# Banded attention in a fused two-layer kernel: three one-pass products of split operands for the projections, their differences on GpSimd, and the turned tiles moved one step ahead

## The reference, cut to what matters

```python
x = x + _L1_attn_b_ref(_layernorm(x), Wqkv, bqkv, Wout, bout)

qkv = (x @ Wqkv.T + bqkv).reshape(B, S, 3, H, d).transpose(2, 0, 3, 1, 4)
q, k, v = (qkv[0], qkv[1], qkv[2])
kp = jnp.pad(k, ((0, 0), (0, 0), (pads, pads), (0, 0)))      # pads = 64
...
scores = jnp.einsum('bhncd,bhnld->bhncl', qc, kb) / np.sqrt(d)
band = (j >= c) & (j < c + WIN)                               # WIN = 128
attn = jax.nn.softmax(jnp.where(band, scores, -jnp.inf), axis=-1)
o = jnp.einsum('bhncl,bhnld->bhncd', attn, vb).reshape(B, H, S, d)
o = o.transpose(0, 2, 1, 3).reshape(B, S, D)
return o @ Wout.T + bout
```

## Time and profile before

| | |
|---|---|
| time, median of 3 runs | 3794.84 us (3794.36 to 3796.17) |
| time of the profiled execution | 3795.73 us |
| its span, first to last instruction | 3793.8 us |
| mean granted TensorE clock | 0.968 of full |
| busy over the span: PE, PEld, DVE, ACT, POOL | 92%, 81%, 62%, 56%, 39% |
| first and last instruction of the changed stage's products | 2896.4 us, 3614.5 us |

### The profile page before, as it was taken

How to read it: one execution, slowest core, us unless ns; L and a number is a source line. 1 busy time by engine, 2 the same in 40 slices (tenths; PEclk the granted TensorE clock), 3 DMA queues, 4 the chain that set the end, 5 groups by cost and what they waited for, 6 DMA issues and landing times. The chain is left out here.

```text
span 3793.8 us, 115662 instructions
## 1 busy us (share of the span) xinstructions
PE 3506.4 (92%) x44514; PEld 3086.2 (81%) x44514; DVE 2371.0 (62%) x6503; ACT 2117.6 (56%) x6528; POOL 1471.5 (39%) x2245
## 2 busy tenths in 40 slices
PE   8948999799839999799999999999998999999998
PEld 7838999677629999798899999999976777777777
DVE  6774555688765554455444444444456888888894
ACT  3345555545446555344444444444444888888895
POOL 3444665210035655344454444444444222222215
PEclk9978999899969999999999999999998999999999
DMA  3143443411153443300000000000000000000002
GB/s 122 42 139 98 93 93 68 135 52 46 63 186 80 93 93 79 88 3 3 3 3 3 3 3 3 3 3 3 3 6 16 2 2 2 2 2 2 2 2 94
DMA packets 137900, 164.61 MB, mean 43 GB/s; under 512 B 11392, under 2 KB 127264, under 8 KB 137376
## 3 DMA queue, kind: packets, MB, share of 16 engines
q1 hardware_dynamic: 112800, 123.81, 10.1%
q0 software_dynamic: 24576, 33.57, 5.3%
HBM read 97.18 MB, written 60.16 MB: 41 GB/s over the span
## 5 line engine op out<-in xcount | busy, mean ns | idle before, releaser
L2290 ACT ACTIVATE wa_S<-wa_S,wa_top 128x256 f32<-128x256 f32 x1024 | 511.8, 507 | 138.8 <-DVE wa_top L2354 137.9
L1912 DVE TENSOR_TENSOR so_raw<-so_rows,so_masks 128x1024 f32<-128x1024 f32 x256 | 313.6, 1225 | 227.9 <-PE so_rows L1612 219.6
L2354 DVE CUSTOM_DVE_ANT_0 wa_S<-wa_bank,wa_band 128x256 f32<-128x256 f32 x1024 | 366.9, 420 | 8.4 <-issue 8.3
L1991 POOL TENSOR_TENSOR so_more<-so_compact,so_head 128x384 f32<-128x384 f32 x224 | 185.5, 828 | 338.3 <-PE so_bankC L1694 307.5
L2213 PE MATMUL wa_bank<-ident,wa_S 128*128 128x128 f32 x2048 | 275.3, 276 | 21.0 <-ACT wa_probT L2297 21.0
L2213 PEld LDWEIGHTS wa_bank<-ident,wa_S 128*128 128x128 f32 x2048 | 231.9, 141 | 65.8 <-ACT wa_S L2290 29.7
L1901 DVE SCALAR_TENSOR_TENSOR so_compact<-so_compact,so_bankX 128x96 f32<-128x96 f32 x192 | 48.9, 255 | 355.5 <-PE so_bankX L1730 355.5
L1828 ACT COPY so_O<-so_bankC 128x128 f32<-128x128 f32 x256 | 68.4, 267 | 307.8 <-PE so_bankC L1694 307.8
L1996 POOL TENSOR_TENSOR so_OT<-so_O,so_OT 128x128 fp32r<-128x128 f32 x256 | 117.5, 459 | 307.3 <-ACT so_OT L1834 307.3
L626 POOL DMA_INDIRECT sum_dram<-y,rows x128 | 223.5, 1746 | 29.4 <-issue 27.2
L704 ACT ACTIVATE m4e_hT<-m_bank,m4e_bias 128x256 fp32r<-128x256 f32 x256 | 126.4, 494 | 153.2 <-PE m_bank L656 146.0
(11 more groups left out here) (452 smaller groups left out, 10171.7 us busy)
## 6 DMA issues: line engine op xcount, KB each, us to landing
m_w_raw<-in_L_ffn_W_dram SPq DMA_DIRECT2D x64, 512.0 KB
sum_dram<-X SPq DMA_DIRECT2D x16, 1024.0 KB, 4.5
X<-sum_dram SPq DMA_DIRECT2D x16, 1024.0 KB, 7.8
X<-in_L_attn_a_x_dram SPq DMA_DIRECT2D x8, 1024.0 KB, 11.3
xn_dram<-m2r_xn SPq DMA_DIRECT2D x16, 512.0 KB, 4.5
sp_gx<-gate_dram SPq DMA_DIRECT2D x64, 128.0 KB, 2.7
xn_dram<-m4r_xn SPq DMA_DIRECT2D x16, 512.0 KB, 4.7
out_dram<-X SPq DMA_DIRECT2D x8, 1024.0 KB, 4.4
```

The source lines that it names most:

```text
L1912: nc.vector.tensor_tensor(AB[:, t % 2].rearrange("p h m t -> p h (m t)"), rows4[:, :, 0:2 * P], masks[:].rearrange("p m t -> p (m t)")[:, ...
L1991: nc.gpsimd.tensor_tensor(state[:, t % UT], compact[:, t % UT, :, None, :].broadcast_to([P, 3, HG, DK]), head[:, None, :, None].broadcast_ ...
L2290: nc.scalar.activation(S[:, n % 2, z], S[:, n % 2, z], ACT.Exp, bias=top[:, n % 2, z:z + 1], scale=-1.0, accum_out=sums[:, i % 2, SET * c ...
L2354: nc.vector.tensor_tensor_reduce(out=S[:, n % 2, z], in0=bS[g][:, eo * SPAN:(eo + 1) * SPAN], in1=band[:], scale=-(D ** -0.5), scalar=3e38 ...
```

## The change

1. The weights `wT` and the turned tiles `xnT` become pairs of fp32r tensors, high part and low part, and each product is the sum of high by high, high by low and low by high: six matmuls of 128x512 per query or key item in place of two fp32 ones, and twelve of 128x256 per value item in place of four.
2. ScalarE makes the high part of a turned item by its copy, and then a second, plain copy of the same bank into `xT_raw`, a single buffer. GpSimd subtracts (`low_xT`), and products wait for `xT_low`.
3. The weights are loaded into `wT_raw`, which lies in the memory of `S`; in the prologue ScalarE makes their high parts in two pieces, and VectorE the low ones.
4. The turned items are now 0, 1, 2 and 6, and the query and key products 3, 4, 5 and 7 to 11.
5. The tile that wraps around is taken whole from an edge that GpSimd copies behind the sequence, so item 15 has no halves.
6. `share_all`, `RT`, `y` and `xT_raw` lie in resident buffers; `share_all` has one buffer in place of two, so that `spread_share(i)` waits for `turn_share(i-1)` (`RT_done`).

```diff
-    ACT_ITEMS, DVE_ITEMS = (0, 1, 6, 7), (2, 3, 4, 5, 8, 9, 10, 11, 12, 13, 14, 15)
+    TURNS, PRODUCTS = (0, 1, 2, 6), (3, 4, 5, 7, 8, 9, 10, 11)
+    ACT_ITEMS, DVE_ITEMS = TURNS, PRODUCTS + (12, 13, 14, 15)
+    PARTS = ((0, 0), (0, 1), (1, 0))
+    XRING = 4
...
-        wT = sb("wT", [P, HC, 3 * HID])
+        wT = sb("wT", [P, 2, HC, 3 * HID], F32R)
+        W_PIECES = (slice(0, 2 * HID), slice(2 * HID, 3 * HID))
...
-        xn, xnT = sb("xn", [P, 4, HID]), sb("xnT", [P, HC, PADDED])
+        xn, xnT = sb("xn", [P, XRING, HID]), sb("xnT", [P, 2, HC, SEQ + EDGE], F32R)
...
+        wT_raw = S[:].rearrange("p a z k -> p (a z k)")[:, 0:HC * 3 * HID].rearrange("p (c r) -> p c r", c=HC)
+        y, xT_raw = R.y[:, 0], R.y[:, 1]
+        share_all, RT = (R.L[:].rearrange("p i e -> p (i e)")[:, n * HID:(n + 1) * HID] for n in range(2))
...
+                def low_xT(p):
+                    m = on_act(p)
+                    pool.wait_ge(s_["act_item"], m + 1)
+                    nc.gpsimd.tensor_tensor(turned_part(1, p), xT_raw, turned_part(0, p).bitcast(F32), ALU.subtract
+                                            ).then_inc(s_["xT_low"], 1)
+                    if p % ITEMS == TURNS[-1]:
+                        pool.wait_ge(s_["xT_low"], m + 1)
+                        nc.gpsimd.tensor_copy(xnT[:, :, :, 0:EDGE], xnT[:, :, :, SEQ:SEQ + EDGE]).then_inc(s_["xT_edge"], 1)
...
-                    if i >= 2:
-                        pool.wait_ge(s_["RT_done"], i - 1)
+                    if i >= 1:
+                        pool.wait_ge(s_["RT_done"], i)
...
-                for i in range(TB + 4):
+                for i in range(4):
                     normalize(i)
+                for m, p in enumerate(TURNS):
+                    if m >= 1 and 2 * m + 3 < TB:
+                        normalize(2 * m + 2)
+                        normalize(2 * m + 3)
+                    low_xT(p)
                 spread_Q(0)
+                for i in range(TB, TB + 4):
+                    normalize(i)
                 for i in range(NT + 2):
+                    b, j = divmod(i, TB)
+                    more = b + 1 < BATCH
+                    after = TB * (b + 1)
+                    if j == 1 and more:
+                        low_xT(ITEMS * (b + 1) + 1)
                     if i + 1 < NT:
                         spread_Q(i + 1)
                     if 2 <= i < NT + 2:
                         residual(i - 2)
                     if 1 <= i <= NT:
                         spread_share(i - 1)
-                    if i + TB + 4 < NT:
-                        normalize(i + TB + 4)
+                    if j in (0, 1, 2, 4) and more:
+                        new = after + {0: 4, 1: 6, 2: TB, 4: TB + 2}[j]
+                        if new < NT:
+                            normalize(new)
+                            normalize(new + 1)
+                    if 2 * j in TURNS and more:
+                        low_xT(ITEMS * (b + 1) + 2 * j)
...
-                    elif k < 12:
-                        half, e = k // 6, (k - 2) % 6
-                        pe.wait_ge(s_["act_item"], on_act(ITEMS * b + (2 if half == 0 else 8)))
+                    elif k in PRODUCTS:
+                        half, e = divmod(PRODUCTS.index(k), 4)
+                        pe.wait_ge(s_["xT_low"], len(TURNS) * b + (2 if half == 0 else 4))
                         at = EDGE + half * HALF
-                        for c in range(HC):
-                            last = nc.tensor.matmul(to[:], wT[:, c, e * P:(e + 1) * P], xnT[:, c, at:at + HALF],
-                                                    start=(c == 0), stop=(c == HC - 1))
+                        steps = [(u, v, c) for u, v in PARTS for c in range(HC)]
+                        for n, (u, v, c) in enumerate(steps):
+                            last = nc.tensor.matmul(to[:], wT[:, u, c, e * P:(e + 1) * P], xnT[:, v, c, at:at + HALF],
+                                                    start=(n == 0), stop=(n == len(steps) - 1))
...
+                    m = on_act(p)
+                    turned = of[:].rearrange("p (a c t) -> p a c t", a=2, c=HC)
+                    nc.scalar.copy(turned_part(0, p).rearrange("p c (a t) -> p a c t", a=2), turned)
+                    if m >= 1:
+                        act.wait_ge(s_["xT_low"], m)
+                    nc.scalar.copy(xT_raw.rearrange("p c (a t) -> p a c t", a=2), turned).then_inc(s_["act_item"], 1)
+
+                def high_w(n):
+                    nc.scalar.copy(wT[:, 0, :, W_PIECES[n]], wT_raw[:, :, W_PIECES[n]]).then_inc(s_["w_high"], 1)
...
+                for n, piece in enumerate(W_PIECES):
+                    dve.wait_ge(s_["w_high"], n + 1)
+                    nc.vector.tensor_tensor(wT[:, 1, :, piece], wT_raw[:, :, piece], wT[:, 0, :, piece].bitcast(F32), ALU.subtract
+                                            ).then_inc(s_["w_ready"], 1)
```

More of the change, by code:

```diff
@@ L2166, in item @@
                         at = EDGE + half * HALF
-                        for c in range(HC):
-                            last = nc.tensor.matmul(to[:], wT[:, c, e * P:(e + 1) * P], xnT[:, c, at:at + HALF],
-                                                    start=(c == 0), stop=(c == HC - 1))
-                    else:
-                        pe.wait_ge(s_["act_item"], on_act(ITEMS * b + 8))
+                        steps = [(u, v, c) for u, v in PARTS for c in range(HC)]
+                        for n, (u, v, c) in enumerate(steps):
+                            last = nc.tensor.matmul(to[:], wT[:, u, c, e * P:(e + 1) * P], xnT[:, v, c, at:at + HALF],
+                                                    start=(n == 0), stop=(n == len(steps) - 1))
+                    else:
+                        pe.wait_ge(s_["xT_low"], len(TURNS) * (b + 1))
+                        steps = [(u, v, c) for u, v in PARTS for c in range(HC)]
+                        if k == ITEMS - 1:
+                            pe.wait_ge(s_["xT_edge"], b + 1)
@@ L2172, in item @@
                         for a in range(2):
-                            block_at = 2 * (k - 12) + 1 + a
+                            block_at = (2 * (k - 12) + 1 + a) % TB
                             cols = slice(a * HID, (a + 1) * HID)
[L2175 to L2183, removed]
+                            for n, (u, v, c) in enumerate(steps):
+                                last = nc.tensor.matmul(to[:, cols], xnT[:, u, c, block_at * P:(block_at + 1) * P], wT[:, v, c, 2 * HID:],
+                                                        start=(n == 0), stop=(n == len(steps) - 1))
@@ L2236, in turn_share @@
                     for c in range(HC):
-                        last = nc.tensor.transpose(bO[:, HID + c * P:HID + (c + 1) * P], share_all[:, i % 2, c * P:(c + 1) * P], R.ident[:])
+                        last = nc.tensor.transpose(bO[:, HID + c * P:HID + (c + 1) * P], share_all[:, c * P:(c + 1) * P], R.ident[:])
                     last.then_inc(s_["RT_done"], 1)
@@ L2246, in _ @@
                 for p in range(ITEMS):
-                    if p == 2:
-                        pe.wait_ge(s_["qkv_loaded"], 16)
+                    if p in (PRODUCTS[0], 12):
+                        pe.wait_ge(s_["w_ready"], 2 if p == 12 else 1)
                     item(p)
@@ L2280, in item @@
                     act.wait_ge(s_["item_done"], p + 1)
-                    at = EDGE + item_tiles(k)[0] * P
-                    nc.scalar.copy(xnT[:, :, at:at + 2 * P].rearrange("p c (a t) -> p a c t", a=2),
-                                   of[:].rearrange("p (a c t) -> p a c t", a=2, c=HC)).then_inc(s_["act_item"], 1)
+                    m = on_act(p)
[6 more added lines that the diff above has]
+                    nc.scalar.copy(wT[:, 0, :, W_PIECES[n]], wT_raw[:, :, W_PIECES[n]]).then_inc(s_["w_high"], 1)
                 def exponent(n, z):
```

50 lines of the change are left out of this document (27 added, 23 removed).

## The result

The changed kernel takes 3774.72 us (median of five runs, 3772.48 to 3779.7) against 3796.17 (3794.36 to 3800.93) for the kernel before on the same chip: a ratio of 0.9944, with a 95% interval of 0.9934 to 0.9955.

What follows compares the result with a forecast made beforehand. Odd product steps were taken as PE's own, even ones as held by a DVE and ACT chain; -0.69 us a sequence, -4.8 over seven, and +0.5 in the prologue gave -4.3, so 3790.5 us, range 3780 to 3801.

Steps and rivals of the forecast that it cites:

- Step 7: Loop step given the moved product: waits 0.88 us for GpSimd's difference, 5.50 to 7.36 us, +1.86 a sequence.
- odd product steps: Odd loop steps 5, 9, 11 and 13, set by PE's own work: 6.99 less 0.30 each, -1.20 us a sequence.
- fourth rival: Slower: GpSimd's difference is late in step 7; 1.7 us later makes the kernel over 0.2% slower; chance 0.06.
- price of an item: PE's saving per split product item: 0.30 us, between 0.24 and 0.37, so an item of 1.42 us.
- the ring: Loop chain of step end, DVE copies and item, masks, ACT exponentials and copies, PE: 5.58 us whatever PE's item costs.
- Even product steps: Five even loop steps with a product: PE alone 5.41 us, held at 5.58, 0.13 saved each, -0.65 a sequence.
- step 38: Even turn step of the earlier trace: 1.29 us less PE work, still 5.58 us, after a wait for ACT.
- second rival: The ring gives way as DVE's and ACT's work moves up with PE's: near 3781 us; chance 0.14.
- Steps 1, 2, 3 and 6: Loop steps: 1 and 2 ACT-bound at 5.84 (+0.47 together), 3 at 6.48 (-0.51), 6 staying at 5.58 us.
- Step 15: Last step of a loop sequence, loses its item's halves too: 7.35 to 6.69 us, -0.66.
- The prologue: Before the loop: items save 3.6 us against later first product and waits; +0.5 us taken, between -2 and +5.

Runs made afterwards that it cites:

- run 3: Changed kernel, but in the loop step 7's product also waits for the difference of item 6's turn, which it does not need; 3780.72 us.
- run 1: Changed kernel with its products back in fp32, the new order, ScalarE's second copy and GpSimd's differences kept; 3806.63 us, ratio 1.0028 to the kernel before.
- run 5: Changed kernel with two of the three products, a third of each item's matmuls left out; 3750.09 us.
- run 4: Changed kernel with split products but the items in the order of before (turns 0, 1, 6, 7); 3791.5 us.
- run 7: Changed kernel with VectorE's statistics moved from the end of odd steps to behind the fourth mask of even steps; 3773.03 us.
- run 8: As run 7, with VectorE's item also written out behind the second mask of the next step; 3759.9 us, ratio 0.9898 to the kernel before.
- run 9: Kernel before (fp32 products) with VectorE's item behind the next step's second mask and statistics behind even steps' fourth; 3780.07 us, ratio 0.996.
- run 2: Changed kernel with fp32 products, without ScalarE's second copy and GpSimd's differences, so the new order alone; 3797.67 us, ratio 1.0004 to the kernel before.
- run 6: Changed kernel without ScalarE's second copy of a turned tile, the difference reading the high part twice (low part zero); 3766.15 us.
- run 10: As run 8, with ScalarE's second copy moved to VectorE behind the next step's third mask; 3758.13 us, ratio 0.9901 to the kernel before.

## Why the prediction was wrong

The forecast for a sequence was -0.69 us and the measured figure -2.52. Of the 1.83 us between them, 0.90 is step 7, 0.96 the five odd product steps, and the rest of the table agrees within 0.02 a step.

- **Step 7 (wrong; 6.3 us over seven sequences).** The step that failed is "Step 7, now a product one step behind its own turn". It is not behind its own turn. The product with k = 7 is the fourth entry of `PRODUCTS`, and so the last one of the first half, which reads the turns of items 0 and 1. The second half starts with k = 8, two steps behind the turn of item 6. The trace shows it directly. This is POOL in step 39:

```profile
3154.90 1.29 POOL L2120 TENSOR_TENSOR wa_xnT<-y,wa_xnT 128x512 fp32r<-128x512 f32 x1 [1.38 <-ACT y L2318]
```

  This difference, of the turn of item 6, ends at 3156.19, and the product has started at 3155.26. The rest of the line, from 5.50 less 0.44 plus the item, gives 6.48, and 6.46 came. The forecast's reading, made real in run 3, costs 1.03 us a sequence. So +1.86 was +0.96, and the wait had a sound price and no place. The fourth rival, slower by a late difference, fell with it: 1.28 us for a difference is hidden everywhere in the loop.

- **The price of an item (a little small).** I took 0.30. With all else equal, run 1 and the changed kernel show 0.32 to 0.33 in steps 3 and 7. By the Trainium skill (FP8 and Floating Point Precision, TensorE Precision Notes) true fp32 takes four passes; three would then be three quarters of 1.72 us, an estimate of 0.43 less. The measured saving stays under it. By run 5 two matmuls of 128x512 are 0.46 us in an odd step, so the six are an estimated 1.4.

- **Odd product steps (wrong; 6.7 us).** "6.99 less 0.30" took PE's saving alone and got 6.69, but 6.50 came. 0.03 is the item's price; 0.16 was not in the sum. It comes from the end of the even step in front. DVE, from the end of step 36:

```profile
3139.49 1.34 DVE L2404 COPY wa_probT<-wa_bank 128x512 f32<-128x512 f32 x2 [0.33 <-PE wa_bank L2245]
3140.74 0.74 DVE L2374 TENSOR_SCALAR wa_Q<-wa_bank,wa_bqk 128x512 f32<-128x512 f32 x1
3141.40 0.24 DVE L2411 RECIPROCAL wa_share<-wa_sums 128x16 f32<-128x16 f32 x1
```

  And the same rows of the kernel before:

```profile
3149.62 1.29 DVE L2362 COPY wa_probT<-wa_bank 128x512 f32<-128x512 f32 x2 [0.66 <-PE wa_bank L2213]
3150.82 0.74 DVE L2332 TENSOR_SCALAR wa_KT<-wa_bank,wa_bqk 128x512 f32<-128x512 f32 x1
3151.48 0.24 DVE L2369 RECIPROCAL wa_share<-wa_sums 128x16 f32<-128x16 f32 x1
```

  The step ends at 3140.03 after and at 3149.95 before. So DVE's copies start 0.54 us ahead of the end of the step, where before it was 0.33, and the reciprocal stands 1.37 us into the next step and not 1.53. POOL spreads the shares (3141.71, 1.68 us in, and 3151.79, 1.84 us in), PE turns them (`turn_share`, 2.13 in place of 2.29), and all that follows in the odd step is 0.16 earlier. Before, PE went through its last turned blocks without a pause, and DVE followed later; now the ring holds the last of them, and DVE gains on PE. Runs 4 and 7 show both states: behind an even step that PE ends without a pause (6.64 or 5.37) `turn_share` starts late and the odd step takes 6.66; behind one held at 5.58 it takes 6.50. That an odd step "is PE's own" was true of its last part only. Its beginning hung on a chain through DVE and POOL that shows no wait on PE, and the forecast took the absence of a wait in the earlier trace rows for the whole answer. The wait does stand in the profile, on PEld. This is the weight load of `turn_share`, of step 37 before and after:

```profile
3152.24 0.20 PEld L2237 LDWEIGHTS wa_bank<-ident,wa_share_all 128*128 128x128 f32 x2 [0.41 <-POOL wa_share_all L2123]
```

```profile
3142.16 0.20 PEld L2269 LDWEIGHTS wa_bank<-ident,L 128*128 128x128 f32 x2 [0.24 <-POOL L L2140]
```

  In runs 8 and 9 `turn_share` starts 2.09 us into the odd product steps (2.23 in step 13 of run 9), and this load waits for POOL nowhere in the loop. The forecast's own numbers held a hint as well: step 7 before, 5.50 less 0.44 plus 1.72, is 6.78, and the odd product steps took 6.99 with the same work on PE. The 0.21 between them is this wait, and run 9 removes it (6.78). The changed kernel shows the exchange once more by itself: ahead of step 4 of sequence 0 VectorE has no statistics yet, and steps 4 and 5 take 5.37 and 6.66 us there.

- **Even product steps (right).** 5.58, with PE held by ACT, as step 38 had said. This is ACT's second copy of step 36:

```profile
3138.76 0.57 ACT L2335 COPY wa_probT<-wa_bank 128x512 f32<-128x512 f32 x1
```

  It ends at 3139.33, and PE's last four turned blocks start at 3139.47. The pause before them is so short that the row of PE shows it only as 1.24 us in place of 1.04. Run 5 confirms the hold: two matmuls fewer, and still 5.58. The second rival, that the ring gives way, did not happen by itself; the ring gives way when VectorE's order is changed (runs 7 and 8).

- **Steps 1, 2, 3 and 6 (right).** 5.84 and 5.84 were forecast and 5.86 twice came; 6.48 and 6.46; 5.58 and 5.58. The second copy is what steps 1 and 2 pay for (runs 2 and 6). Step 15 (6.69, and 6.49 came) is as the odd ones.

- **The prologue (sign wrong, inside its bounds).** +0.5 us was taken between -2 and +5, and -1.52 came. These are PE's first products, which answer to the earlier trace rows:

```profile
2898.04 6.05 PE L2203 MATMUL wa_bank<-wa_xnT,wa_wT 128*128 128x512 f32 x18 [0.63 <-POOL wa_xnT L2120]
...
2907.12 5.74 PE L2203 MATMUL wa_bank<-wa_xnT,wa_wT 128*128 128x512 f32 x24 [1.20 <-POOL wa_xnT L2120]
...
2918.25 1.15 PE L2228 MATMUL wa_bank<-wa_KT,wa_QM 32*128 32x256 f32 x16
```

  The first product starts 14.5 us into the stage, 10.6 before: 3.9 later, where 3.2 had been worked out. The wait after item 6 is 1.20 us. Before it was 0.82, as the first row below shows, so it grew by 0.38 and not by 1.5: item 7 does not wait for that difference here either, and PE does it in the meantime. The items, from the first product to the first scores, take 20.21 us where it was 25.61, 5.4 us less, and the forecast had 3.6 less 1.5. Run 1 has the same order with fp32 products; its rows come second:

```profile
2907.91 7.11 PE L2168 MATMUL wa_bank<-wa_xnT,wa_wT 128*128 128x512 f32 x16 [0.82 <-ACT wa_xnT L2282]
```

```profile
2898.51 7.37 PE L2203 MATMUL wa_bank<-wa_xnT,wa_wT 128*128 128x512 f32 x12 [0.63 <-POOL wa_xnT L2120]
2905.71 0.60 PE L2196 MATMUL wa_bank<-ident,wa_xn 128*128 128x128 f32 x4
...
2908.91 7.10 PE L2203 MATMUL wa_bank<-wa_xnT,wa_wT 128*128 128x512 f32 x16 [0.88 <-DVE wa_KT L2374]
...
2922.85 1.15 PE L2228 MATMUL wa_bank<-wa_KT,wa_QM 32*128 32x256 f32 x16
```

  That is 24.34 us, so the split itself gives 4.13 of the 5.4, 0.34 an item. The granted clock was low (0.54 in 2898 to 2902, in the changed kernel) during most of the first three products, which save 0.44 each (7.20 to 5.89 us for three); at 1.00 the next four of their kind save 0.34. The other 1.27 us come with the new order, the whole last item and the later start, and no run separates these.

- **Sequence 0 and the end (not in the sum).** Sequence 0 gains 3.47 us, 0.9 more than the others, mostly in steps 1 and 2 (6.36 and 5.70 us there, then 6.43 and 5.29), and what follows step 112 is 0.79 shorter. The first has no measured cause; the second is within the scatter of that part.

With step 7 (6.3), the odd steps (6.7), the prologue (2.0), sequence 0 and the end (0.9 and 0.8) and the start of the stage (2.2) the sum goes from the -4.3 forecast to -23.2; the two spans differ by 23.3.

## What to carry to other kernels

Before pricing a wait, work out from the loop's indices which iteration the waiting instruction really depends on: one wrong step of dependence was here a third of the error, although its price was nearly right. In a loop whose engines hand over to one another a step without a wait on PE is still set by when its parts could begin (look at PEld's waits too): write down, for each step, how late the chain that opens it runs, and ask how that moves when the step in front becomes shorter or gets held. Where a step's length doesn't answer to the bound engine's work (run 5), reorder the queue of the engine that feeds it: putting VectorE's item and statistics behind the first masks took the ratio from 0.9944 to 0.9898.

## What the runs showed of the hardware

A VectorE subtraction with two SBUF inputs takes longer where a GpSimd one runs. These are two rows of DVE in the prologue of the changed kernel, and POOL at that time:

```profile
2892.32 1.16 DVE L2432 TENSOR_TENSOR wa_wT<-wa_S,wa_wT 128x1024 fp32r<-128x1024 f32 x1
2896.76 1.68 DVE L2432 TENSOR_TENSOR wa_wT<-wa_S,wa_wT 128x512 fp32r<-128x512 f32 x1 [3.28 <-ACT wa_wT L2321]
```

```profile
2890.80 3.56 POOL L2114 TENSOR_SCALAR wa_xn<-X,rstd,shift 128x256 f32<-128x256 f32 x4 [3.80 <-DMA wa_pick<-in_pick_dram]
...
2895.57 1.10 POOL L2114 TENSOR_SCALAR wa_xn<-X,rstd,shift 128x256 f32<-128x256 f32 x2
2896.62 1.27 POOL L2120 TENSOR_TENSOR wa_xnT<-y,wa_xnT 128x512 fp32r<-128x512 f32 x1
```

The second subtraction has half the columns of the first and took 1.68 us, the first 1.16. It ends at 2898.44, 0.55 us after POOL's difference (2897.89), as if it had run only then. POOL's four normalised tiles beside the first one took 3.56 us, where two take 1.10.

Two runs show the same subtraction at another moment. First DVE in run 2, where GpSimd makes no difference:

```profile
2896.86 0.78 DVE L2426 TENSOR_TENSOR wa_wT<-wa_S,wa_wT 128x512 f32<-128x512 f32 x1 [2.80 <-ACT wa_wT L2315]
```

Then DVE and POOL in run 10, where the difference began 0.23 us behind it:

```profile
2897.03 0.78 DVE L2438 TENSOR_TENSOR wa_wT<-wa_S,wa_wT 128x512 fp32r<-128x512 f32 x1
```

```profile
2897.26 1.67 POOL L2121 TENSOR_TENSOR wa_xnT<-y,wa_xnT 128x512 fp32r<-128x512 f32 x1
```

So 512 columns take 0.78 us here and 1.68 beside POOL's difference, and in run 10 it is the difference that takes longer, 1.67 us in place of 1.27. Even the 0.78 us are not free of POOL: in both runs a normalised tile of POOL ends within them (at 2897.10 and at 2897.27), and the subtraction ends 0.54 us later. That agrees with the Trainium skill (SBUF — State Buffer, Who interferes with whom), by which such a VectorE instruction and a GpSimd one that reads SBUF shut each other out, a rule that the prediction found no row for. These rows come from runs made for other ends; none was made to separate the two engines.
